# The entries of two expert mixtures laid out partition by partition, and the last addition moved into the expert tiles' block

## The reference

```python
x = x + _L0_attn_ref(_layernorm(x), ...)      # 16 heads of 64, tanh clamp, causal
x = x + _L0_ffn_ref(_layernorm(x), ...)       # 8 experts, top 1, relu, 128 -> 512 -> 128
x = x + _L1_attn_ref(_layernorm(x), ...)      # 16 heads of 8, rope, causal by pages of 32
x = x + _L1_ffn_ref(_layernorm(x), ...)       # 8 experts, top 2, swiglu, and a shared swiglu
```

```python
y = y + comb[:, e:e + 1] * _swiglu(xt, w1[e], w2[e], w3[e])
```

## Time and profile before

| What | us |
|---|---|
| device time, median of 3 runs | 1947.33 |
| lowest and highest run | 1945.76, 1948.58 |
| span of the profiled execution | 1942.0 |
| its own device time | not recorded beside its span |
| busy: PE, PE weight loads | 1723.3 (89%), 1029.1 (53%) |
| busy: DVE, ACT, POOL | 1364.9 (70%), 1229.6 (63%), 507.7 (26%) |
| last scatter of results issued | at 1909.44 |
| first load of layer 1's entries issued | at 1911.82 |
| first load of layer 0's entries issued | at 1011.73 |

### The profile page before, as it was taken

How to read it: one execution, slowest core, us unless ns; L and a number is a source line. 1 busy time by engine, 2 the same in 40 slices (tenths; PEclk the granted TensorE clock), 3 DMA queues, 4 the chain that set the end, 5 groups by cost and what they waited for, 6 DMA issues and landing times. The chain is left out here.

```text
span 1942.0 us, 35641 instructions
## 1 busy us (share of the span) xinstructions
PE 1723.3 (89%) x12164; PEld 1029.1 (53%) x12164; DVE 1364.9 (70%) x2932; ACT 1229.6 (63%) x1752; POOL 507.7 (26%) x813
## 2 busy tenths in 40 slices
PE   5999999999999999993966499999999999669993
PEld 3556655666566556652963134343334343439992
DVE  6677677777777777774548598888888884245664
ACT  5888888878888888771655236666665667214443
POOL 1221121223121411131441112222512424133441
PEclk9999999999999999996988679999999999789996
DMA  5111111101111101103223513231311310312225
GB/s 180 50 39 39 39 36 39 37 25 49 39 36 39 47 26 39 36 24 133 62 79 131 183 32 55 39 61 32 83 32 42 73 32 14 124 33 57 60 61 146
DMA packets 101189, 115.66 MB, mean 60 GB/s; under 512 B 15467, under 2 KB 75212, under 8 KB 100397
## 3 DMA queue, kind: packets, MB, share of 16 engines
q1 hardware_dynamic: 94454, 100.22, 18.7%
q0 software_dynamic: 6592, 13.56, 2.1%
HBM read 78.86 MB, written 34.41 MB: 58 GB/s over the span
## 5 line engine op out<-in xcount | busy, mean ns | idle before, releaser
L1724 ACT ACTIVATE a_p<-a_score 128x1024 f32<-128x1024 f32 (+3 forms) x384 | 302.5, 810 | 218.6 <-PE a_score L1746 212.2
L1852 DVE TENSOR_REDUCE a_mx<-a_misc 128x1 f32<-128x512 f32 (+3 forms) x768 | 380.3, 549 | 45.7 <-PE a_misc L1779 33.5
L306 ACT ACTIVATE a_p<-a_score 128x1024 f32<-128x1024 f32 (+3 forms) x384 | 292.6, 816 | 36.3 <-PE a_score L343 35.2
L248 POOL TENSOR_SCALAR_AFFINE_SELECT a_p<-a_p 128x256 f32<-128x256 f32 x256 | 125.8, 521 | 640.9 <-ACT a_p L324 640.9
L1776 PE MATMUL a_misc<-a_k,a_q 72*128 72x512 bf16 (+3 forms) x768 | 251.7, 348 | 30.4 <-DVE a_out L1970 22.0
L324 ACT ACTIVATE a_p<-a_p 128x2560 f32<-128x2560 f32 (+1 forms) x128 | 273.9, 2140 | 1.1
L362 PE MATMUL a_out<-a_p,a_v 128*64 128x512 f32 (+3 forms) x1536 | 269.9, 493 | 0.0
L343 PE MATMUL a_score<-a_q,a_k 64*128 64x512 f32 (+3 forms) x2304 | 266.7, 361 | 3.1 <-ACT a_p L306 1.5
L1746 PE MATMUL a_score<-a_q,a_k 128*128 128x512 bf16 (+3 forms) x768 | 234.1, 330 | 6.8 <-ACT a_p L1724 6.6
L343 PEld LDWEIGHTS a_score<-a_q,a_k 64*128 64x128 f32 x2304 | 185.6, 186 | 85.0 <-issue 41.2
L522 DVE TENSOR_TENSOR a_part<-a_part,a_p 128x1024 f32<-128x1024 f32 (+3 forms) x256 | 223.6, 873 | 7.7 <-ACT a_p L324 0.9
(11 more groups left out here) (301 smaller groups left out, 2613.8 us busy)
## 6 DMA issues: line engine op xcount, KB each, us to landing
a_xt<-xt SPq DMA_DIRECT2D x31, 512.0 KB, 3.4
a_q<-qk_parts SPq DMA_DIRECT2D x144, 64.0 KB
a_k<-qk_parts SPq DMA_DIRECT2D x144, 64.0 KB
e_xs<-f_x_rows SPq DMA_DIRECT2D x110, 64.5 KB, 1.8
qk_parts<-p_part SPq DMA_DIRECT2D x24, 256.0 KB, 6.4
xt<-a_p SPq DMA_DIRECT2D x9, 512.0 KB, 3.6
a_w<-in_l_attn_w SPq DMA_DIRECT2D x32, 128.0 KB, 3.1
values<-xt_all SPq DMA_DIRECT2D x4, 1024.0 KB, 7.3
```

The costliest lines, as they stand in the source:

```text
L248: last = nc.gpsimd.affine_select(out=blk, in_=blk, compare_op=ALU.is_ge, fill=0.0, base=0, pattern=[[0, 2], [1, P]], channel_multiplier=-1)
L306: nc.scalar.activation(chunk_of(prob[p], c), score_ps[:, c % 2, :, 0:width], ACT.Tanh, scale=scale / clamp).then_inc(tanh_done, 1)
L1724: nc.scalar.activation(prob[s % RING][:, :, 0:width], score_ps[:, s % 2, :, 0:width], ACT.Exp, scale=scale).then_inc(exp_done, 1)
L1852: nc.vector.tensor_reduce(m[c][:, h, t:t + 1], misc[:, bank, 0:keys], AX_X, ALU.max).then_inc(free, 1)
```

## The change

The entry of token t*128 + p in batch b is now b*1024 + p*8 + t. So the entries of one partition stand side by side in memory, 8 x 512 bytes = 4 KB, and the loads of a batch read one run of 4 KB for each partition. The numbers are no longer read from the input for this: POOL makes them in `pool_make` with an iota and a copy to float, and DVE waits for those (`made`, 5) in place of the loaded ones. The input still carries the numbers of the blank rows, for which ACT in layer 0 now waits itself. The scatters write the same rows of 512 bytes, in other places. The output is stored as before, in runs of 512 bytes.

`Entries` is taken apart into functions that run inside the block of `expert_tiles`, behind each engine's last step; its own block is gone.

```diff
+def entry_rows(nc, pool, whole, rows, made, at):
+
+
+    nc.gpsimd.iota(whole[:], pattern=[[SEQ, BATCH], [1, TILES]], base=0, channel_multiplier=TILES).then_inc(made, 1)
+    pool.wait_ge(made, at + 1)
+    nc.gpsimd.tensor_copy(rows[:], whole[:]).then_inc(made, 1)
...
                                 pattern=[[1, P]], channel_multiplier=-1).then_inc(made, 1)
+        entry_rows(nc, pool, self.entry_whole, self.entry_rows, made, 3)
...
-        dve.wait_ge(sems["loaded"], 16 * 3)
-        V.tensor_copy(self.xn[b % 2][:, :, D], self.numbers[:, b * TILES:(b + 1) * TILES]).then_inc(sems["numbered"], 1)
+        dve.wait_ge(sems["made"], 5)
+        V.tensor_copy(self.xn[b % 2][:, :, D], self.entry_rows[:, b * TILES:(b + 1) * TILES]).then_inc(sems["numbered"], 1)
...
                 act.wait_ge(blank_made, 1)
+                act.wait_ge(routes.sems["loaded"], 16 * 3)
                 nc.scalar.copy(blank[:, :, D], routes.numbers[:, ALL_TILES:ALL_TILES + BLANKS]).then_inc(blank_made, 1)
...
                 for b in range(BATCH):
-                    sp.dma_start(got[b], entries_dram[b * SEQ:(b + 1) * SEQ, :].rearrange("(t p) d -> p t d", p=P))\
+                    sp.dma_start(got[b], entries_dram[b * SEQ:(b + 1) * SEQ, :].rearrange("(p t) d -> p t d", t=TILES))\
                         .then_inc(arrived[b], 16)
...
-        dve.wait_ge(self.sems["loaded"], 16 * 3)
+        dve.wait_ge(self.sems["made"], 5)
         for c in range(2):
-            self.nc.vector.tensor_scalar(self.xn[b][c][:, :, D], self.numbers[:, b * TILES:(b + 1) * TILES], float(c * TOKENS),
+            self.nc.vector.tensor_scalar(self.xn[b][c][:, :, D], self.entry_rows[:, b * TILES:(b + 1) * TILES], float(c * TOKENS),
...
-                if load_entries is not None:
+                if entries is not None:
                     for r in range(XS):
                         sp.wait_ge(stored[r], 16 * ((N + XS - 1 - r) // XS))
-                    load_entries(sp)
+                    entries.sp_load(sp)
+                    entries.sp_store(sp)
...
             @block.scalar
             def _(act):
                 steps(act, act_step)
+                if entries is not None:
+                    entries.act_weigh(act)
 
             @block.vector
             def _(dve):
                 steps(dve, dve_step)
+                if entries is not None:
+                    entries.dve_add(dve)
...
-    def load(self, sp):
+    def sp_load(self, sp):
         for b, c in self.parts:
-            at = (c * ALL_TILES + b * TILES) * P
-            sp.dma_start(self.got[b][c][:], self.entries_dram[at:at + SEQ, :].rearrange("(t p) d -> p t d", p=P))\
+            at = c * TOKENS + b * SEQ
+            sp.dma_start(self.got[b][c][:], self.entries_dram[at:at + SEQ, :].rearrange("(p t) d -> p t d", t=TILES))\
                 .then_inc(self.arrived[b, c], 16)
...
-    def add(self, x, weights, out):
-        nc, got = self.nc, self.got
-        with nc.Block() as block:
...
+    def sp_store(self, sp):
+        for b in range(BATCH):
+            sp.wait_ge(self.added, b + 1)
+            sp.dma_start(self.out[b].rearrange("(t p) d -> p t d", p=P), self.x[:, b * TILES:(b + 1) * TILES, :])\
+                .then_inc(self.stored, 16)
+        sp.wait_ge(self.stored, 16 * BATCH)
...
-                     entries.load)
-        entries.add(x, weights, out)
+                     entries)
```

More of the change, by code:

```diff
@@ L756, in __init__ @@
         self.numbers = kit.sb(f"{tag}_numbers", [P, ALL_TILES + tiles])
+        self.entry_whole, self.entry_rows = kit.sb(f"{tag}_entry_whole", [P, ALL_TILES], I32), kit.sb(f"{tag}_entry_rows", [P, ALL_TILES])
         self.stats, self.mv = kit.sb(f"{tag}_stats", [P, TILES, 6]), kit.sb(f"{tag}_mv", [P, TILES, 2])
@@ L2234, in expert_tiles @@
 def expert_tiles(nc, kit, sem, tag, ident, N, tile_expert, tile_source, wa_all, wb_all, NC, gated, biased, x_rows, y_entries,
-                 load_entries=None):
+                 entries=None):
     E, A = wa_all.shape[1:]
@@ L2425, in _, with __init__ @@
                 steps(dve, dve_step)
+                if entries is not None:
+                    entries.dve_add(dve)
 class Entries:
-    def __init__(self, nc, kit, sem, tag, entries_dram):
-        self.nc, self.entries_dram = nc, entries_dram
+    def __init__(self, nc, kit, sem, tag, entries_dram, x, weights, out):
+        self.nc, self.entries_dram, self.x, self.weights, self.out = nc, entries_dram, x, weights, out
         self.parts = [(b, c) for b in range(BATCH) for c in range(2)]
@@ new lines, in sp_store, with act_weigh @@
+    def sp_store(self, sp):
[4 more added lines that the diff above has]
+        sp.wait_ge(self.stored, 16 * BATCH)
+    def act_weigh(self, act):
+        for b in range(BATCH):
+            act.wait_ge(self.arrived[b, 1], 16)
+            for t in range(TILES):
+                at = ALL_TILES + b * TILES + t
+                self.nc.scalar.activation(self.got[b][1][:, t, :], self.got[b][1][:, t, :], ACT.Copy,
+                                          scale=self.weights[:, at:at + 1]).then_inc(self.weighed, 1)
@@ new lines, in dve_add @@
+    def dve_add(self, dve):
+        V, x, got = self.nc.vector, self.x, self.got
+        for b in range(BATCH):
+            dve.wait_ge(self.arrived[b, 0], 16)
+            for t in range(TILES):
+                at = b * TILES + t
+                V.scalar_tensor_tensor(x[:, at, :], got[b][0][:, t, :], self.weights[:, at:at + 1], x[:, at, :],
+                                       ALU.mult, ALU.add).then_inc(self.first_added, 1)
+            dve.wait_ge(self.first_added, (b + 1) * TILES)
+            dve.wait_ge(self.weighed, (b + 1) * TILES)
+            to = x[:, b * TILES:(b + 1) * TILES, :]
+            V.tensor_tensor(to, to, got[b][1][:], ALU.add).then_inc(self.added, 1)
@@ L2517, in ffn1 @@
                            tile_expert, tile_source, shared)
-        entries = Entries(nc, k, sem, "add1", y_entries)
+        entries = Entries(nc, k, sem, "add1", y_entries, x, weights, out)
         expert_tiles(nc, k, sem, "e1", ident, N, tile_expert, tile_source, wa_all, wb_all, NC, True, False, x_rows, y_entries,
-                     entries.load)
-        entries.add(x, weights, out)
+                     entries)
 def transformer_kernel(nc, x_in, l0_attn_w, gate0, gate0_bias, starts0, numbers0, wa_0, wb_0,
```

27 lines of the change are left out of this document (removed).

## The result

| What | before | after |
|---|---|---|
| median over 20 runs each, us | 1943.25 | 1934.98 |
| lowest to highest | 1936.43 to 1950.86 | 1926.84 to 1951.28 |
| ratio (95% interval) | | 0.9965 (0.9948 to 0.9981) |
| profiled execution: device time, us | not recorded | 1930.12 |
| profiled execution: span, us | 1942.0 | 1928.3 |

A forecast was written before the change was run, and what follows sets the result against it. PE, busy for 89% of the span, was taken as the bound, so only stretches where PE waits could pay: -7.0 at the end and -1.1 at the hand-over, 1947.33 - 8.1 = 1939.2 us, 8 in 10 between 1936.6 and 1943.0.

The forecast's parts named there:

- The base: Whole kernel: the median of three runs, 1947.33 us, taken as the time from which the 8.1 us are subtracted.
- The range: Whole kernel: 8 in 10 between 1936.6 and 1943.0 us, with 2 us each way for the clock in layer 1.
- The end: Layer 1's entry additions after the expert tiles: no wait for SP's issuing, last addition at 1930.4 against 1937.34, -7.0 us.
- The hand-over: Between the layers, four loads of layer 0's entries in 4 KB runs: DVE's first addition earlier, -1.1 us, passing through layer 1's projection.
- Rival B: Layer 1's projection: another chain or TensorE's clock sets the pace, the -1.1 is lost; 1940.3 us, chance 0.15.
- POOL's constants: New iota and copy on POOL, twice: free, since POOL idles and DVE reads the numbers much later; cost 0.
- The scatters: Expert stages, result rows at new addresses: at most 0.3 us more per landing, which fits into DVE's slack; cost 0.
- Rival C: Expert stages: scatters to new addresses get slower; landings longer by 1 us cost 14.7 us, 1953.9 us, chance 0.04.
- Rival A: Entry loads: 512 B runs already at full rate, only the removed wait counts; -4.9 us, 1942.4 us, chance 0.10.
- Rival D: First additions on DVE or ACT late for another reason (code fetch, slower issue); 3 us lost, 1942.2 us, chance 0.06.
- The sum: Whole kernel: -7.0 at the last additions and -1.1 between the layers, -8.1 us, giving 1939.2 us; chance 0.65.

## Why the prediction was right or wrong

- **The base, the step that failed.** "1947.33 - 8.1 = 1939.2" took the median of three runs as the kernel's time. Those runs lay within 2.8 us of each other and looked like a narrow thing. Twenty runs span 14.4 us, and their median is 4.1 lower. 1943.25 - 8.1 would have given 1935.2 beside the measured 1934.98; that they agree so closely is luck, since the ratio leaves the gain open between 3.7 and 10.1 us. A sign was there: "so 5.3 us lie around the span" made the difference between the median and one execution's span a fixed cost. It is 1.8 us, and the other 3.5 said that this execution was faster than the three.
- **The range, the same error.** "Plus 2 us each way for what the clock makes of a shifted phase" was read from those three runs, and was too small; the result lies 1.6 us below the range. Over the 20 runs of the changed kernel the time goes with the mean granted clock (correlation -0.92): about 2.4 us for each 0.001, from 1925.0 us of span at 0.948 to 1949.5 at 0.939. The later sets of either kernel show 1.5 to 2.7 us and correlations of -0.76 to -0.88.
- **The end, -7.0 forecast, -6.74 in the trace.** Right by its steps. The first part was used after 3.66 us (3.4 taken), further parts came 1.38 apart (1.29), the last addition ended 18.80 us after the first issue (18.6 by my times), and DVE's own pace was the bound, 3.35 us (3.36).
- **How the 6.74 divide.** Alone, the long runs give 5.05 (30.18 - 25.13) and the one block 5.10 (30.18 - 25.08): together less than their sum, since both attack the same wait for SP's 11 us of issuing. Each leaves about 1.7 of the 6.74 behind, one for POOL's drain, the other for the pace of the parts. The drain was in no step of mine; it cost the forecast nothing only because the one block hides it.
- **The hand-over, -1.1 forecast, -1.16 in the trace.** The start of DVE's addition is shown three times over (3.97, 4.02 and 4.18 against 5.13, and 5.23 with short runs). That the shift "reaches its end" isn't shown. r_full came 94.53, 94.58 and 95.49 us after the first load's issue in the three kernels with short runs, and after 93.02, 93.44, 96.42, 95.85, 94.88 and 94.67 in the six profiles with long runs and no transposes: means of 94.9 and 94.7, and a scatter wider than the gain. Rival B is therefore neither confirmed nor ruled out; it would change the time by 1.1.
- **POOL's constants, 0 forecast.** The iota took 0.16 us and the copy 0.21. Nothing waited.
- **The scatters, 0 forecast.** Landings still take 2.2 us, and DVE's waits for them are 9.7 to 10.2 us in the changed kernel's three profiles, 9.9 with the old addresses and 11.9 before. Rival C is out.
- **Rival A** (512 B runs at full rate already) is out. Parts of short runs came 1.8 us apart with the block gone, those of 4 KB runs 1.38: 289 and 380 GB/s. (The 405 GB/s taken from other transfers was a little high.) The rule of the Trainium skill's "DMA: Bandwidth & Descriptors" (Specifications), 512 B for line rate, doesn't hold in this trace.
- **Rival D** is out: both first additions came within 0.3 us of the forecast.
- **The sum.** 6.74 + 1.16 = 7.9 in the trace. The three ratios, 0.9965, 0.9968 and 0.9954, give 6.8, 6.2 and 8.9 us of 1943; 7.9 is inside each interval.

## What to carry to other kernels

Before a saving is subtracted from a median, ask what the median rests on: three runs that agree within 0.15% don't show a spread of 0.7%, and a profiled span that doesn't fit them by the usual distance is a fourth run that says so. What a throttled clock makes of the rest can be wider than the gain. To judge a small change, measure the stretch that it touches, from one event to the next, and take one in which nothing waits for throttled work. And where engines meet, look for who comes second: a wait removed uncovers the next one, which here was POOL's drain, long hidden by SP's issues. A mean over a group can hide that as well: 538 ns were 29 instructions of 344 ns and three of 2.4 us.

## What the runs showed of the hardware

- POOL's drain at the end of a block in which it only scatters takes longer the more scatters it has issued since its last: 0.71, 1.37, 3.24 and 5.85 us after 8, 16, 39 and 71, although all have landed (0.29 us where drains stand in the tiles). 3.24 of the 7.13 us between layer 0's last scatter and the first load of its entries are this. In blocks where POOL also computes it is longer (3.6, 9.9, and 2.2 with no scatter), and the trace doesn't say why. Paying it earlier shrank the gap (4.19 and 4.28 us) and gained nothing, since a drain between scatters took 2.65 to 3.45 us with three or four scatters behind it, and 4.42 with 34.
- A load of 128 runs of 4 KB took SP 0.33 to 0.43 us to issue at the hand-over and 0.45 in the median over the end's eight; one of 1024 runs of 512 B took 0.39 as the first of eight and up to 2.0 later on.
- While POOL added over 128x1024, a DVE multiply-add on other tiles (two inputs in SBUF) stood until POOL was done: 2.43 us in place of 0.34, once for each of three additions.
- The transposes at the head of the projection put off DVE's first addition: 5.31, 5.46, 5.31 and 5.59 us after the first issue in the four kernels that have them, 3.97 to 4.18 in those without and with long runs. In ten microseconds from 1009 on, one of the former shows a transfer of instructions that the changed kernel doesn't (below); that it is the cause, by standing ahead of the entries on one of the DMA engines, was not tried.

```profile
q8 instruction: 1, 0.02, 1.0%
```
